# Splitting one product into a keys' and a values' product, and moving the keys' product between two groups of transposes

## What is computed

```python
qp = q @ Wq.T
kp = k @ Wk.T            # k and v are both ctx_1024
vp = v @ Wv.T
kp = _rope(kp)
vp = _rope(vp)
scores = jnp.einsum('bhqd,bhkd->bhqk', qh, kh) / jnp.sqrt(jnp.float32(dh))
weights = jax.nn.softmax(scores, axis=-1)
ctx = jnp.einsum('bhqk,bhkd->bhqd', weights, vh)
x = x + jnp.tanh(g_xattn[0]) * (ctx @ Wp.T + bp)
x = x + jnp.tanh(g_ffn[0]) * _L0_ffn_ref(_layernorm(x, axis=-1), ...)
```

## Time and profile before

| | |
|---|---|
| median of 3 runs | 569.37 us (568.95 to 570.17) |
| the profiled execution | 569.16 us |
| span of its instructions | 567.4 us |
| share of the span in which PE / DVE / ACT / POOL are busy | 95% / 71% / 73% / 67% |
| granted PE clock, mean of the span | 0.983 |

### The profile page before, as it was taken

How to read it: one execution, slowest core, us unless ns; L and a number is a source line. 1 busy time by engine, 2 the same in 40 slices (tenths; PEclk the granted TensorE clock), 3 DMA queues, 4 the chain that set the end, 5 groups by cost and what they waited for, 6 DMA issues and landing times.

```text
span 567.4 us, 20235 instructions
## 1 busy us (share of the span) xinstructions
PE 538.1 (95%) x5964; PEld 457.0 (81%) x5965; DVE 401.5 (71%) x1356; ACT 411.9 (73%) x1083; POOL 378.5 (67%) x520
## 2 busy tenths in 40 slices
PE   8999999999999999999999998799999999999960
PEld 6888887788887887887887878699999999999950
DVE  5888988898998899899899865433333333335763
ACT  4788888888888888889998885356666666666630
POOL 3236777767767677776776767777766666666770
PEclk9999999999999999999999999899999999999995
DMA  3832121121212212122221124333333333337997
GB/s 88 239 121 75 55 81 58 56 74 61 79 56 71 68 51 79 56 61 72 68 76 56 52 69 143 104 100 109 98 93 93 93 93 94 94 90 208 314 317 222
DMA packets 70246, 57.96 MB, mean 102 GB/s; under 512 B 8966, under 2 KB 66062, under 8 KB 70192
## 3 DMA queue, kind: packets, MB, share of 16 engines
q1 hardware_dynamic: 52672, 35.98, 22.3%
q0 software_dynamic: 8640, 16.93, 9.0%
q10 hardware_dynamic: 8880, 4.39, 2.6%
HBM read 29.84 MB, written 24.15 MB: 95 GB/s over the span
## 4 chain that ended last, share of the span: by engine, by line
PE 86%; issue 4%; POOL 3%; DMA 2%; DVE 2%; ACT 1%; POOLq 0%; SPq 0%; ACTq 0%; DVEq 0%
PE psH L548 18%; PE psO L520 12%; PE psH L460 11%; PE psH L446 7%; PE psH L452 7%; PE psK L498 5%; PE psO L562 5%; PE psG L562 4%; PE psO L478 3%; PE psX L465 3%; PE psO L492 3%; POOL results L1134 2%; PE psX L502 1%; PE psK L473 1%; PE psX L503 1%
## 5 line engine op out<-in xcount | busy, mean ns | idle before, releaser
L1134 POOL DMA_INDIRECT results<-ys,zin x142 | 141.9, 999 | 55.1 <-issue 51.0
L1085 POOL DMA_INDIRECT lists<-zp,dest x128 | 128.5, 1004 | 62.5 <-DVE dest L889 32.6
L548 PE MATMUL psH<-zT,wcur 128*128 128x256 f32 x568 | 136.0, 383 | 0.0
L548 PEld LDWEIGHTS psH<-zT,wcur 128*128 128x128 f32 x568 | 103.3, 192 | 11.4
L994 DVE TENSOR_TENSOR hm<-psH,hs 128x512 f32<-128x512 f32 x71 | 49.1, 692 | 85.9 <-PE psH L548 51.4
L627 ACT ACTIVATE ex<-psH,rs 128x512 f32<-128x512 f32 x128 | 81.2, 684 | 39.0 <-PE psH L452 39.0
L874 DVE TENSOR_REDUCE mx<-psH 128x8 fp32r<-128x512 f32 x128 | 82.4, 686 | 4.5 <-PE psH L446 0.3
L520 PEld LDWEIGHTS psO<-v,pT 128*64 128x64 f32 x2048 | 64.9, 138 | 25.1 <-issue 23.1
L460 PE MATMUL psH<-ident,ex 128*128 128x128 f32 x512 | 76.5, 282 | 0.1
L520 PE MATMUL psO<-v,pT 128*64 128x64 f32 x2048 | 73.7, 225 | 0.6 <-ACT pT L631 0.6
L1116 POOL TENSOR_TENSOR kvr<-ropA,ropB 128x256 f32<-128x256 f32 x64 | 46.5, 726 | 40.3 <-DVE ropB L951 24.0
(11 more groups left out here) (157 smaller groups left out, 991.6 us busy)
## 6 DMA issues: line engine op xcount, KB each, us to landing
zin<-lists SPq DMA_DIRECT2D x71, 130.0 KB, 2.1
yy<-results SPq DMA_DIRECT2D x16, 512.0 KB, 5.5
xres<-x1r SPq DMA_DIRECT2D x32, 128.0 KB, 2.2
out_dram<-xres ACTq DMA_DIRECT2D x16, 256.0 KB, 3.6
xring<-in_x_dram SPq DMA_DIRECT2D x31, 128.0 KB, 2.2
cring<-in_ctx_dram SPq DMA_DIRECT2D x31, 128.0 KB, 2.4
results<-ys,zin POOLq DMA_INDIRECT x142, 2.3
lists<-pad SPq DMA_DIRECT2D x16, 130.0 KB, 2.5
```

The lines of the kernel that those rows point to most:

```text
L548: last = pe.matmul(bank[t.buf(2)][:, k * ET:(k + 1) * ET], wcur[:, t.buf(2), a, k * P:(k + 1) * P], zT[:, t.buf(2), :], start=True, stop=True)
L1085: nc.gpsimd.indirect_dma_start(lists, bass.IndirectOffsetOnAxis(ap=dest[:, t.buf(4), j:j + 1], axis=0), zp[:, t.buf(4), j, :], None).then_ ...
L1134: nc.gpsimd.indirect_dma_start(results, bass.IndirectOffsetOnAxis(ap=zin[:, t.buf(8), h, D:D + 1].bitcast(U32), axis=0), ys[:, t.buf(8), h ...
```

## The change

The product of 256 columns becomes two of 128 columns with the same stationary operand. The keys' product goes between `turn(t, 1)` and `turn(t, 0)` and takes both waits along; the values' product stays behind the output projection, without a wait of its own, and counts up `kv_ps`.

```diff
                     if t := ATT_PE.at(s, 2):
                         wait_for(pe, exp_done[1], t)
                         turn(t, 1)
+                    if t := ATT_PE.at(s, 4):
+                        if static(s, -3):
+                            busy(3)
+                        wait_for(pe, xc_sb, t)
+                        wait_for(pe, k_sb, t, back=1)
+                        pe.matmul(psK[:, 0:D], xcT[:, t.buf(8), P:2 * P], wT[:, 1, :], start=True, stop=True)
                     if t := ATT_PE.at(s, 2):
                         wait_for(pe, exp_done[0], t)
                         turn(t, 0)
...
                     if t := ATT_PE.at(s, 4):
-                        if static(s, -3):
-                            busy(3)
-                        wait_for(pe, xc_sb, t)
-                        wait_for(pe, k_sb, t, back=1)
-                        pe.matmul(psK[:, 0:2 * D], xcT[:, t.buf(8), P:2 * P], wT[:, 1:3, :], start=True, stop=True).then_inc(kv_ps, 1)
+                        pe.matmul(psK[:, D:2 * D], xcT[:, t.buf(8), P:2 * P], wT[:, 2, :], start=True, stop=True).then_inc(kv_ps, 1)
```

## The result

The changed kernel takes **587.6 us** (median of 4, 586.1 to 588.5) against 569.5 us (median of 4) for the kernel before: the ratio is 1.0315, with a 95% interval of 1.029 to 1.034. The prediction was 584.2 with a range of 577 to 592. The span of the profiled execution grew from 567.4 to 585.5 us, by 18.1.

A forecast was written before the change was run, and what follows sets the result against it. PE's chain of steps was taken as the bound. Eight tiles lose 1.86 us, 0.23 a tile, 14 us over 60 tiles; with 1 us for ACT on 569.16 this gave 584.2 us, range 577 to 592.

The forecast's parts named there:

- The wait on the masking: Before the moved keys' product: PE asks for `k_sb` at 0.44 us instead of 1.26, too early in seven of eight tiles.
- K: Time in a step from PE's first transpose to the end of DVE's masking; read as 0.37 to 1.11 us.
- the 0.12 us to the load: At the moved keys' product: its load starts 0.12 us after the masking ends.
- the restart: At the moved keys' product: 0.11 us extra with an empty array, so the fifth transpose starts at K + 0.45.
- K + 1.34: Forecast start in the step of the input transpose L502, against 1.70 or 1.76 us before the change.
- The split costs nothing: Two added loads per tile at the split products should be hidden: priced 0.01 us a tile, taken as nothing.
- The old hole: Between fourth and fifth transpose, loads idle 0.16 us until the exponential of half 0 is done; forecast to disappear.
- The rival in which the product fills the hole: Between the transpose groups: product fills the idle time, -0.15 us a tile, 560 us; chance 0.03.
- K 0.37: not held to speak of: Tile with the earliest masking: L502 at 1.61 against 1.76 us, at best -0.15, taken as -0.10.
- K should keep its size: DVE's masking follows PE's own work, so the time to its end should not shrink when PE slips.
- The sum: Losses over a cycle of eight tiles: 1.86 us, 0.23 a tile, 14 us over 60 tiles.
- ACT's lateness: In eight tiles where ACT scales experts' weights, q's product waits for `xcT`: 8 x 0.15, about 1 us.
- Does the loss repair itself: Asked whether DVE gains on PE in later steps and shrinks the loss; the forecast answered that it doesn't.

The follow-up runs named there:

- The wait alone: Kernel before with only the wait for the masking moved between the two groups of transposes, product whole at its old place: 580.1 us, ratio 1.0175.
- kernel without the tie: Changed kernel with DVE masking untransposed keys from SBUF, keys' product without the masking wait, POOL given one: 662.9 us, ratio 0.9999, on a chip with stalls.
- the first four runs: Split only, 570.15 us; masking wait only, 580.1; changed kernel with masking first on DVE, 586.86; split with keys' product behind half 0, 573.1; kernel before 569.7.

## Why the prediction was right

The time came out 3 us above the forecast, inside its range, and by the mechanism that was forecast. Per tile the terms were close, and where they were off they were mostly too low.

- **The wait on the masking** was the cause, with K, the 0.12 us to the load, the restart and K + 1.34 as read the earlier trace rows. The wait alone costs 10.4 us; asked later, with the product, it costs 3.4 or nothing. That the rest of the 18 comes from the product's restart is worked out from single tiles, not from a run of its own. That nothing but the wait makes the moved product lose is seen in the tiles ahead of the stalls: 5.16 to 5.17 us with it, 4.93 to 4.94 without, on both of the other chips.
- **The split costs nothing**: shown.
- **The old hole is gone, and the wait stands in its place**: shown in ordinary tiles; over the kernel the loads' idle time released by the exponential fell from 10.1 to 1.9 us. The rival in which the product fills the hole has the right mechanism for a kernel without the tie, though its 0.15 us a tile was 0.09 in undisturbed ones; with the tie it never came.
- **"K 0.37: not held to speak of"** was wrong. The masking ends before the four transposes do, and yet they don't hide the restart; the tile gives 0.01 in place of -0.10. The 1.61 forecast for its input transpose is what a tile of this kind has without the wait (kernel without the tie, step from 248.17); with the wait it is 1.70, by K + 1.34.
- **"K should keep its size"** was off by 0.04 in ordinary tiles, which made their term 0.15 in place of 0.10. The stretch behind the input transpose did keep its length, 5.02 - 1.70 = 3.32 before and 5.16 - 1.84 = 3.32 after, but its pieces shifted. The chain of the changed kernel for that tile:

```profile
205.46 0.28 PE psO L478 x2
...
207.91 0.66 PE psH L446 x16
...
210.63 0.27 PE psO L478 x2
```

  In the chain of the kernel before, in the tile of the earlier trace rows, the scores (L446) took 0.62 and L478 0.32. The scores are 0.04 us longer, since the loads of half 0 now spread: 0.28 us for sixteen against 0.23. The second copy of probabilities, which they wait for, ends at 207.86, after their first load at 207.84. That is the likely reason, and no run undid it. L478 is 0.04 to 0.05 shorter. The masking starts 0.31 behind L473 in ordinary tiles of both kernels, and L473 now stands 0.49 in place of 0.54 ahead of the first transpose, so K is 0.50 in place of 0.46.
- **The sum.** Over a cycle of eight tiles, 206.10 to 246.47 before and 216.06 to 258.56 after, the loss is 2.13 us where the terms gave 1.86. The ordinary tiles, with 0.20, and the tile of K 0.37, with 0.11, are most of that; the late ones cost 0.07 less than forecast, as their K fell from 1.11 and 1.00 to 1.07 and 0.95. And the product meets transposes in 62 tiles, not 60: 62 x 2.13 / 8 = 16.5 us for the 14 of the forecast.
- **ACT's lateness** was named as a price of 1 us in the tiles with the scalings. The wait for `xcT` is there, eight times, 1.7 us in all. With the 16.5 this makes 18.2, where the span grew by 18.1.
- **"Does the loss repair itself"**: it didn't; K is within 0.05 of what it was, but for two late tiles in the stretch with the scalings, where it fell from 1.07 to 0.81 and from 1.17 to 0.96.

## What to carry to other kernels

A hole in front of a wait can be filled only with work whose own inputs are ready by then: put the release time of each wait that moves on the same axis as the new place, for each kind of tile, since the fourth tile can cost more than the other three. A release that comes just before the place isn't enough: here a release 0.07 us ahead of it still put the restart on PE's path. A wait for another engine that only guards a shared PSUM bank is a wait like any other; before an instruction is moved, see whether its neighbour in the bank can live elsewhere (the Trainium skill, page "PSUM — Partial Sum Buffer", Terms, calls two engines in one bank and quadrant at once an error, so the wait can't just be dropped; no run here shows that). And where the late thing is behind other work on its engine, moving it forward makes that work late: follow what is queued behind it before counting the gain.

## What the runs showed of the hardware

- PE restarts more cheaply with transposes than with a float32 product: four transposes from their first load took 0.50 us for 0.44 streaming, a product of 256 columns 0.54 for 0.43, one of 128 columns 0.33 for 0.22 (206.31 to 206.64 in the changed kernel).
- The restart behind a wait isn't hidden by work that is still streaming in front of it: with the masking done 0.07 us before the four transposes were through (K 0.37), the next group started at K + 0.44, as in tiles where PE stood waiting (K + 0.45).
- On the two other chips the kernel before took 93 and 112 us longer than on the chip of the first four runs, with stalls for an unnamed releaser from about 44 us on. There the wait between the two groups of transposes cost 6.4 us (669.3 against 662.9, both masking from SBUF), where the change cost 18 on a chip without the stalls.
